# A DeepFM and CIN scorer on one core: six row buffers, gathers that wait for buffers alone, and three lookups instead of four in half of the tiles

## The chip, the cores and the metric

The kernel runs on one core of a Trainium2 chip. The metric is the device time of one execution in microseconds (us), the median of several runs. TensorE (PE in the profile), VectorE (DVE), ScalarE (ACT), GpSimd (POOL) and the DMA queues of SyncE (SP) work side by side and meet at semaphores.

## The reference

For each of 2048 samples there are 26 fields with an index each; an index picks a row of 16 numbers (`emb`) and one weight (`w1`) from the field's table of 12500 rows. Three scores are added:

```
emb = embed_table[f, x_idx]                      # 2048 x 26 x 16
lin1 = w1_table[f, x_idx].sum(1) + w1_bias
s = emb.sum(1);  fm = 0.5 * ((s*s).sum(-1) - (emb*emb).sum((1, 2)))
h = relu(emb.reshape(n, 416) @ mlp_w1 + mlp_b1)  # 416 -> 400
h = relu(h @ mlp_w2 + mlp_b2);  mlp_out = h @ mlp_w3 + mlp_b3
x0 = emb.transpose(0, 2, 1);  last = x0
for W in (cin_w0, cin_w1, cin_w2):               # 128 maps each
    last = einsum('ndl,ndf,klf->ndk', last, x0, W);  feats.append(last)
cin_result = concatenate(feats, -1).sum(1) @ lin_w + lin_b
out = lin1 + fm + mlp_out + cin_result           # 2048 x 1
```

## The kernel before

**Setup.** The three CIN layers are linear in their weights, so the kernel folds them with `lin_w` into one set of small matrices before it looks at any sample. This takes the first 80 us or so, with weight loads, small matmuls and round trips through DRAM.

**Tiles.** The 2048 samples are 16 tiles of 128, one sample to a partition. A tile needs its 26 rows of 17 numbers in `emb[t % EMB]`, with `EMB = 3` such buffers. They get there in two ways.

- *Gathers.* POOL issues one indirect DMA for each tile and field (L500), 128 rows each. Tiles 0 and 1 gather all 26 fields, tiles 2 to 15 the first 22: 360 gathers. The loop waits in three places. In tiles 0 and 1 some gathers wait for steps of the setup (`SETUP_STEPS`). From tile 3 on the first gather of a tile waits until the tile that held the buffer before has been copied (`by_pos_ready`) and its first-order weights summed (`row_sums`, ScalarE's L549 in `sum_first`). And from tile 2 on every second gather waits for `hi_ready`, a count of ScalarE's squares, so that tile t's gathers are spread over the units of tile t - 3 (`PER_UNIT`).
- *Lookups.* The last four fields of tiles 2 to 15 aren't gathered. Their whole tables lie in SBUF, 98 rows to a partition, split into a high and a low part (`look_hi`, `look_lo`, made in tile 0 by L617 and L923). For one lookup VectorE makes a one-hot matrix from the keys (L935), TensorE multiplies it with the tables in eight matmuls (L1197, L1198) into `ps_y`, and VectorE masks the right row (L946) and sums it into `emb` (L950). There are 56 lookups.

**A tile's compute.** ScalarE copies the 26 rows to `by_pos` (L568; for the last tile in parts, L556 and L561), TensorE transposes them in two halves (`x_half`), and then come 12 units, three to each of four quarters. In a unit TensorE forms sums of pairs of fields (`picked`, L1097), ScalarE squares them (L591, L598), VectorE takes the low part (L803), and TensorE multiplies three times (`main`, L1111 to L1113). The two layers of the MLP lie in between. Each engine has one queue, and its order is written out by hand in `tile(t)` and `start_tile(t)`. The position copy of tile t + 1 stands before unit 10 of tile t.

**Where the lookups stand.** A tile's compute has four slots for lookups: TensorE's part at units 0, 3, 6 and 9, VectorE's pick three units later, at units 3, 6 and 9 and in the next `start_tile`. `look_at(t, slot)` numbers the lookups through, shifted by `LATER = 2`: slots 0 and 1 of tile t hold fields 2 and 3 of tile t + 1, slots 2 and 3 hold fields 0 and 1 of tile t + 2. A pick into a buffer waits for the same two semaphores as the gathers.

Of the kernel before, what the change touches and what calls it, by code (L numbers as in the profile page):

```python
# [32 lines left out]
LOOKS = 4  # L33
FIRST_LOOK = 2
LATER = 2
EARLY = 18
PER_UNIT = 2
COLS = 98
WIDE = 26
SHARES = 4  # L40
# [57 lines left out]
def deepfm_cin_kernel(nc, x_idx, rows, w1_bias, mlp_w1, mlp_b1, mlp_w2, mlp_b2, mlp_w3, mlp_b3,  # L98
                      cin_w0, cin_w1, cin_w2, lin_w, lin_b, out):
    N, F = x_idx.shape  # L100
# [5 lines left out]
    T = N // P  # L106
# [13 lines left out]
    NC = 3  # L120
# [20 lines left out]
    with ExitStack() as ctx:  # L141
        def sb(name, shape, dt=F32):
            return ctx.enter_context(nc.sbuf_tensor(name, shape, dt))
# [4 lines left out]
        def sem(name):  # L148
            return ctx.enter_context(nc.semaphore(name))
# [16 lines left out]
        idx_wrap = sb("idx_wrap", [P, T, F])  # L166
        row_base = sb("row_base", [P, F], I32)
        row_ix = idx_raw
        EMB = 3
        emb = [sb(f"emb{t}", [P, F, R]) for t in range(EMB)]  # L170


# [152 lines left out]
        gathered_late = sem("gathered_late")  # L325
        by_pos_ready = sem("by_pos_ready")
        filled = sem("filled")
        hi_ready = sem("hi_ready")
# [19 lines left out]
        def s_no(t, u):  # L348
            return NPROD * t + NX + u

        def looks(t):

            return LOOKS if FIRST_LOOK <= t < T else 0

        def look_no(t, i):
            return LOOKS * (t - FIRST_LOOK) + i

        def look_at(t, slot):

            n = LOOKS * t + slot - LATER  # L360
            return (FIRST_LOOK + n // LOOKS, n % LOOKS) if 0 <= n < look_no(T, 0) else None

        def looked_by(t):

            return min(max(LOOKS * t + 1 - LATER, 0), look_no(T, 0))


        LOOK_SPLIT = {3: 0, 5: 1, 7: 2, 9: 3}
# [114 lines left out]
        @block.gpsimd  # L483
        def _(pool):
            pool.iota(row_base[:], pattern=[[V, F]], base=0, channel_multiplier=0).then_inc(base_ready, 1)
            SETUP_STEPS = {16: (m_done, 1), 22: (b_done, 1), 34: (s_blocks, 1), 41: (by_row_done, 1), 47: (za_done, 1)}
            for t in range(T):
                if t < 2:
                    pool.wait_ge(ix_ready, t + 1)
                if t >= EMB:  # L490
                    pool.wait_ge(by_pos_ready, 2 * (t - EMB + 1))
                    pool.wait_ge(row_sums, t - EMB + 1)
                for f in range(F - looks(t)):
                    if F * t + f in SETUP_STEPS:
                        signal, value = SETUP_STEPS[F * t + f]
                        pool.wait_ge(signal, value)
                    if t >= EMB - 1 and f and f % PER_UNIT == 0:
                        behind = s_no(t - EMB, NC + f // PER_UNIT - 1) if t >= EMB else s_no(0, f // PER_UNIT)
                        pool.wait_ge(hi_ready, behind + 1)
                    pool.indirect_dma_start(emb[t % EMB][:, f, :], None, rows,  # L500
                                            bass.IndirectOffsetOnAxis(row_ix[:, t, f:f + 1], 0)
                                            ).then_inc(gathered[t] if t < T - 1 or f < EARLY else gathered_late, 16)

# [16 lines left out]
        def _(act):  # L520
# [31 lines left out]
            def copy_last_early():  # L552
                act.wait_ge(gathered[T - 1], 16 * EARLY)
                act.wait_ge(looked, look_no(T - 1, LOOKS))
                for fs in (slice(0, EARLY), slice(F - LOOKS, F)):
                    act.activation(by_pos[:, :, fs], emb[(T - 1) % EMB][:, fs, 0:D].rearrange("p f d -> p d f"), ACT.Copy)  # L556

            def copy_last_late():
                fs = slice(EARLY, F - LOOKS)
                act.wait_ge(gathered_late, 16 * (F - LOOKS - EARLY))  # L560
                act.activation(by_pos[:, :, fs], emb[(T - 1) % EMB][:, fs, 0:D].rearrange("p f d -> p d f"),  # L561
                               ACT.Copy).then_inc(by_pos_ready, 2)

            def copy_by_position(t):
                act.wait_ge(gathered[t], 16 * (F - looks(t)))
                if looks(t):
                    act.wait_ge(looked, look_no(t, LOOKS))
                act.activation(by_pos[:], emb[t % EMB][:, :, 0:D].rearrange("p f d -> p d f"),  # L568
                               ACT.Copy).then_inc(by_pos_ready, 2)
# [54 lines left out]
            def tile(t):  # L624
                for u in range(NC, NU):
                    if u == NU - 2 and t + 1 < T - 1:
                        copy_by_position(t + 1)
                    square(t, u)
                    if u == NU - 1 and t + 1 == T - 1:
                        copy_last_early()  # L630
                        copy_last_late()
                    if t == 0 and u in LOOK_SPLIT:
                        look_high(LOOK_SPLIT[u])
                    if t == 0 and u == 8:
                        second_high()
                    if u == 5:
                        hidden1(t)
                    if u == 7:
                        hidden1_high(t)
# [75 lines left out]
        def _(dve):  # L715
# [148 lines left out]
            def tile(t):  # L864
                for u in range(NC, NU):
                    q = u // NC - 1
                    if u % NC == 2:
                        times_left(t, q)
                    z_low(t, u)
                    if u == NU - 1 and t + 1 < T - 1:  # L870
                        x_low(t + 1, 0)
                    if u % NC == 2 and q:
                        add_product(t, q)
                    if u == 7:
                        hidden1_low(t)
                    if t == 0 and u - 2 in LOOK_SPLIT:
                        look_low(LOOK_SPLIT[u - 2])
                    if t == 0 and u == 10:
                        second_low()
                    if u in PICKED and look_at(t, PICKED[u]):  # L880
                        pick_row(*look_at(t, PICKED[u]))
                    if u in KEYS and look_at(t, KEYS[u]):
                        keys_to_one_hot(*look_at(t, KEYS[u]))
# [15 lines left out]
            def start_tile(t):  # L899
                if look_at(t - 1, LOOKS - 1):  # L900
                    pick_row(*look_at(t - 1, LOOKS - 1))
                x_low(t, 1)
                z_low(t, 0)
                if look_at(t, 0):
                    keys_to_one_hot(*look_at(t, 0))
                z_low(t, 1)
                times_third(t - 1)
                add_third(t - 1)
                times_left(t - 1, NQ - 1)
                z_low(t, 2)  # L910
                hidden2(t - 1)
                add_product(t - 1, NQ - 1)
                fold(t - 1)
# [10 lines left out]
                                  ALU.subtract).then_inc(look_lo_ready, 1)  # L924

            def keys_to_one_hot(t, i):
                if i == 0 and t == FIRST_LOOK:
                    dve.wait_ge(keys_first_in, 16)
                elif i == 0 and t in (FIRST_LOOK + 1, FIRST_LOOK + 3):
                    dve.wait_ge(keys_in[(t - FIRST_LOOK) // 2], 16)  # L930
                n = look_no(t, i)
                keys = key_first[:, i:i + 1, :] if t == FIRST_LOOK else key_row[:, t - FIRST_LOOK - 1, i:i + 1, :]
                if n >= 2:
                    dve.wait_ge(rows_out, n - 1)
                dve.tensor_tensor(one_hot[n % 2][:], keys.to_broadcast([P, SHARES, P]),  # L935
                                  share_row.unsqueeze(2).to_broadcast([P, SHARES, P]),
                                  ALU.is_equal).then_inc(one_hot_ready, 1)
# [84 lines left out]
        def _(pe):  # L1022
# [103 lines left out]
            def sum_products(t):  # L1126

                if looked_by(t + 1):
                    pe.wait_ge(looked, looked_by(t + 1))
                pe.wait_ge(folds, t + 1)  # L1130
                pe.matmul(ps_y[:, YCOL + t:YCOL + t + 1], folded[0:NROW, :], ones[0:NROW, :],
                          start=True, stop=True).then_inc(y_done, 1)
# [173 lines left out]
```

## Time and profile before

| | |
|---|---|
| time, median of 3 runs | 512.84 us (511.73 to 513.11) |
| span of the profiled execution | 694.2 us |
| the profiled execution's own time | its span; no other is given |
| mean granted TensorE clock | 0.863 of full speed |
| POOL | 356.6 us busy, 360 gathers |
| TensorE, VectorE, ScalarE | 510.3, 412.8 and 389.0 us busy |

The profile is one execution, and its span is longer than the timed runs. In its rows L12 is line 12 of the kernel; "idle before" is the engine's own idle time, with the instruction that ended it, and "remote" stands where the releasing instruction wasn't found near the semaphore's update. PE's starts and ends are partly modelled.

### The profile page before, as it was taken

Reading aid. Unit: us, or ns where it says so; the run is one execution under the profiler, and the core shown is the slowest. Engines: PE = TensorE matmul, PEld = TensorE weight load, DVE = VectorE, ACT = ScalarE, POOL = GpSimd, SP = SyncE. Lnnn points to the kernel's source line nnn. Section 1 sums busy time; section 2 is a strip of 40 time slices with the busy share of each in tenths; the row PEclk is TensorE's granted clock in tenths of the full one; section 3 lists DMA queues with packets and bytes.
Section 4 is the critical chain, followed back from the end, with each engine's and each line's share of the span. In section 5 each row is a group of like instructions: output and inputs, shape, how many; then the busy total and the mean of one; then the engine's idle time right before and its main releaser. Section 6 shows DMA issues by size and latency. Waiting matters only on the chain.

```text
span 694.2 us, 6825 instructions
## 1 busy us (share of the span) xinstructions
PE 510.3 (74%) x2235; PEld 415.1 (60%) x2235; DVE 412.8 (59%) x680; ACT 389.0 (56%) x759; POOL 356.6 (51%) x365
## 2 busy tenths in 40 slices
PE   2897918824696959588695959596886949599988
PEld 2865705723484838476574747475765737478666
DVE  6431227903475748376584847484765848478866
ACT  0321628604464847376574847484665748378875
POOL 6665666774465464637466454547374664510000
PEclk9995666975896979979798989899797979899999
DMA  8836434221111111202111111112021111100000
GB/s 176 163 21 117 88 62 103 7 7 5 5 6 7 4 6 4 7 4 8 5 6 5 5 6 6 6 4 8 3 9 5 6 5 5 6 3 1 0 1 0
DMA packets 21508, 15.57 MB, mean 22 GB/s; under 512 B 12790, under 2 KB 19811, under 8 KB 21347
## 3 DMA queue, kind: packets, MB, share of 16 engines
q0 software_dynamic: 11520, 3.16, 13.5%
q1 hardware_dynamic: 6949, 9.99, 5.9%
q10 hardware_dynamic: 3005, 2.01, 1.4%
q8 instruction: 18, 0.29, 0.2%
q14 instruction: 16, 0.12, 0.1%
HBM read 14.92 MB, written 0.21 MB: 22 GB/s over the span
## 4 chain that ended last, share of the span: by engine, by line
PE 28%; DVE 24%; another core or an unknown queue 18%; ACT 15%; issue 11%; DMA 3%; SPq 0%; DVEq 0%
DVE z_lo L803 5%; ACT ps_s L598 5%; ACT z_hi L591 4%; PE ps_y L1197 4%; PE ps_y L1198 3%; DVE ps_y L946 3%; DVE one_hot L935 3%; PE ps_s L1097 2%; DMA w_space<-cin_w 2%; DVE sums L829 2%; PE ps_q L1111 2%; ACT room_a L597 2%; DVE ps_q L814 2%; DVE emb L950 2%
## 5 line engine op out<-in xcount | busy, mean ns | idle before, releaser
L500 POOL DMA_INDIRECT emb<-rows,idx_raw x360 | 356.3, 990 | 253.7 <-issue 101.4
L803 DVE TENSOR_TENSOR z_lo<-ps_s,z_hi 128x512 fp32r<-128x512 f32 (+1 forms) x192 | 132.1, 688 | 138.9 <-ACT ps_s L598 87.6
L591 ACT ACTIVATE z_hi<-ps_s 128x512 fp32r<-128x512 f32 (+1 forms) x192 | 114.2, 595 | 171.9 <-remote 105.6
L1197 PE MATMUL ps_y<-look_hi,one_hot 128*128 128x442 f32 x224 | 92.6, 413 | 91.4 <-DVE one_hot L935 89.6
L598 ACT ACTIVATE ps_s<-ps_s 128x512 f32<-128x512 f32 (+1 forms) x192 | 113.5, 591 | 0.7
L1111 PE MATMUL ps_q<-z_lo,zw_hi 128*127 128x512 f32 (+1 forms) x192 | 86.9, 453 | 32.6 <-DVE z_lo L803 21.1
L1197 PEld LDWEIGHTS ps_y<-look_hi,one_hot 128*128 128x128 f32 x224 | 49.5, 221 | 101.0 <-DVE emb L950 57.1
L1198 PE MATMUL ps_y<-look_lo,one_hot 128*128 128x442 f32 x224 | 89.3, 400 | 0.0
L946 DVE SCALAR_TENSOR_TENSOR ps_y<-tables,look_place,ps_y 128x442 f32<-128x442 f32 x56 | 37.9, 677 | 78.6 <-remote 70.6
L1097 PE MATMUL ps_s<-xt,pick 128*128 128x512 f32 (+1 forms) x192 | 77.1, 414 | 8.6 <-ACT x L582 5.4
L1113 PE MATMUL ps_q<-z_hi,zw_hi 128*127 128x512 f32 (+1 forms) x192 | 78.9, 411 | 0.0
L1112 PE MATMUL ps_q<-z_hi,zw_lo 128*127 128x512 f32 (+1 forms) x192 | 78.9, 411 | 0.0
L1111 PEld LDWEIGHTS ps_q<-z_lo,zw_hi 128*127 128x127 f32 (+1 forms) x192 | 38.2, 199 | 54.9 <-issue 34.4
L1198 PEld LDWEIGHTS ps_y<-look_lo,one_hot 128*128 128x128 f32 x224 | 50.1, 224 | 4.6
L1097 PEld LDWEIGHTS ps_s<-xt,pick 128*128 128x128 f32 (+1 forms) x192 | 37.4, 195 | 18.9 <-issue 5.8
L574 ACT ACTIVATE xt<-ps_s 52x512 fp32r<-52x512 f32 x32 | 18.7, 592 | 45.4 <-remote 17.1
L1113 PEld LDWEIGHTS ps_q<-z_hi,zw_hi 128*127 128x127 f32 (+1 forms) x192 | 38.0, 198 | 9.4
L597 ACT ACTIVATE room_a<-ps_s 128x512 f32<-128x512 f32 x63 | 37.4, 593 | 5.9 <-DVE sums L814 5.9
L1112 PEld LDWEIGHTS ps_q<-z_hi,zw_lo 128*127 128x127 f32 (+1 forms) x192 | 38.5, 200 | 2.6
L593 ACT ACTIVATE z_hi<-ps_s 26x512 fp32r<-26x512 f32 x64 | 37.9, 592 | 0.8
L935 DVE TENSOR_TENSOR one_hot<-w_space,tables 128x512 fp32r<-128x512 f16 x52 | 36.1, 694 | 0.0
L950 DVE TENSOR_REDUCE emb<-ps_y 128x17 f32<-128x442 f32 x56 | 34.7, 619 | 1.9
(191 smaller groups left out, 765.0 us busy)
## 6 DMA issues: line engine op xcount, KB each, us to landing
emb<-rows,idx_raw POOLq DMA_INDIRECT x360
w_space<-rows SPq DMA_DIRECT2D x2, 728.9 KB
m_space<-rows SPq DMA_DIRECT2D x2, 728.9 KB
w_space<-key_scratch SPq DMA_DIRECT2D x1, 1408.0 KB
w<-cin_w SPq DMA_DIRECT2D x2, 416.0 KB, 4.8
w<-cin_w ACTq DMA_DIRECT2D x2, 416.0 KB, 7.6
w_space<-cin_w SPq DMA_DIRECT2D x2, 416.0 KB
w_space<-cin_w ACTq DMA_DIRECT2D x2, 416.0 KB
```

Source lines behind the costliest of these rows:

```text
L500: pool.indirect_dma_start(emb[t % EMB][:, f, :], None, rows, bass.IndirectOffsetOnAxis(row_ix[:, t, f:f + 1], 0)).then_inc(gathered[t] if ...
L591: act.activation(z_hi[0:k, c, :], ps[0:k, :], ACT.Square)
L598: act.activation(ps[0:k, :], ps[0:k, :], ACT.Square).then_inc(hi_ready, 1)
L803: z = dve.tensor_tensor(z_lo[0:k, u % NC, :], ps, z_hi[0:k, u % NC, :].bitcast(F32), ALU.subtract)
L935: dve.tensor_tensor(one_hot[n % 2][:], keys.to_broadcast([P, SHARES, P]), share_row.unsqueeze(2).to_broadcast([P, SHARES, P]), ALU.is_equa ...
L946: dve.scalar_tensor_tensor(by_place, place.unsqueeze(2).to_broadcast([P, WIDE, R]), look_place[:, t, i:i + 1], by_place, ALU.is_equal, ALU ...
L1097: pe.matmul(ps[0:CK[c], :], pick[:, e, c * P:c * P + CK[c]], xt[t % 2][:, 4 * h:4 * h + 4, :], start=True, stop=True).then_inc(filled, 1)
L1111: pe.matmul(ps, hi_w, lo_x, start=(c == 0), stop=False)
L1112: pe.matmul(ps, lo_w, hi_x, start=False, stop=False)
L1113: mm = pe.matmul(ps, hi_w, hi_x, start=False, stop=(c == NC - 1))
L1197: pe.matmul(o, one_hot[n % 2][:, j, :], look_hi[i][:, ws], start=(j == 0), stop=False)
L1198: mm = pe.matmul(o, one_hot[n % 2][:, j, :], look_lo[i][:, ws], start=False, stop=(j == SHARES - 1))
```

## The change

Three edits:

- `EMB` goes from 3 to 6, so a buffer is used again six tiles later. The waits for `by_pos_ready` and `row_sums` follow it (`t >= EMB`, `t - EMB + 1`), in the gathers and in the picks.
- The wait for `hi_ready` before every second gather is gone, with `PER_UNIT`.
- `looks(t)` is 3 for tiles 8 to 15 (`FEWER_FROM = 8`). Field 0 of the four is gathered there as a 23rd field; slot 2 of tiles 6 to 13 stays empty. The other slots hold what they held. There are now 368 gathers and 48 lookups. The functions that number lookups are rewritten for it, and the last tile's copies follow `looks(T - 1)`.

```diff
--- before.py
+++ after.py
@@ -33,8 +33,8 @@
 LOOKS = 4
 FIRST_LOOK = 2
 LATER = 2
+FEWER_FROM = 8
 EARLY = 18
-PER_UNIT = 2
 COLS = 98
 WIDE = 26
 SHARES = 4
@@ -166,7 +166,7 @@
         idx_wrap = sb("idx_wrap", [P, T, F])
         row_base = sb("row_base", [P, F], I32)
         row_ix = idx_raw
-        EMB = 3
+        EMB = 6
         emb = [sb(f"emb{t}", [P, F, R]) for t in range(EMB)]
 
 
@@ -350,19 +350,26 @@
 
         def looks(t):
 
-            return LOOKS if FIRST_LOOK <= t < T else 0
+            return 0 if not FIRST_LOOK <= t < T else LOOKS if t < FEWER_FROM else LOOKS - 1
+
+        def first_field(t):
+            return LOOKS - looks(t)
+
+        LOOK_SEQ = [(t, i) for t in range(FIRST_LOOK, T) for i in range(first_field(t), LOOKS)]
 
         def look_no(t, i):
-            return LOOKS * (t - FIRST_LOOK) + i
+            return len([x for x in LOOK_SEQ if x < (t, i)])
 
         def look_at(t, slot):
 
             n = LOOKS * t + slot - LATER
-            return (FIRST_LOOK + n // LOOKS, n % LOOKS) if 0 <= n < look_no(T, 0) else None
+            look = (FIRST_LOOK + n // LOOKS, n % LOOKS)
+            return look if n >= 0 and look in LOOK_SEQ else None
 
         def looked_by(t):
 
-            return min(max(LOOKS * t + 1 - LATER, 0), look_no(T, 0))
+            n = max(LOOKS * t + 1 - LATER, 0)
+            return look_no(FIRST_LOOK + n // LOOKS, n % LOOKS)
 
 
         LOOK_SPLIT = {3: 0, 5: 1, 7: 2, 9: 3}
@@ -494,9 +501,6 @@
                     if F * t + f in SETUP_STEPS:
                         signal, value = SETUP_STEPS[F * t + f]
                         pool.wait_ge(signal, value)
-                    if t >= EMB - 1 and f and f % PER_UNIT == 0:
-                        behind = s_no(t - EMB, NC + f // PER_UNIT - 1) if t >= EMB else s_no(0, f // PER_UNIT)
-                        pool.wait_ge(hi_ready, behind + 1)
                     pool.indirect_dma_start(emb[t % EMB][:, f, :], None, rows,
                                             bass.IndirectOffsetOnAxis(row_ix[:, t, f:f + 1], 0)
                                             ).then_inc(gathered[t] if t < T - 1 or f < EARLY else gathered_late, 16)
@@ -552,12 +556,12 @@
             def copy_last_early():
                 act.wait_ge(gathered[T - 1], 16 * EARLY)
                 act.wait_ge(looked, look_no(T - 1, LOOKS))
-                for fs in (slice(0, EARLY), slice(F - LOOKS, F)):
+                for fs in (slice(0, EARLY), slice(F - looks(T - 1), F)):
                     act.activation(by_pos[:, :, fs], emb[(T - 1) % EMB][:, fs, 0:D].rearrange("p f d -> p d f"), ACT.Copy)
 
             def copy_last_late():
-                fs = slice(EARLY, F - LOOKS)
-                act.wait_ge(gathered_late, 16 * (F - LOOKS - EARLY))
+                fs = slice(EARLY, F - looks(T - 1))
+                act.wait_ge(gathered_late, 16 * (F - looks(T - 1) - EARLY))
                 act.activation(by_pos[:, :, fs], emb[(T - 1) % EMB][:, fs, 0:D].rearrange("p f d -> p d f"),
                                ACT.Copy).then_inc(by_pos_ready, 2)
 
@@ -924,9 +928,9 @@
                                   ALU.subtract).then_inc(look_lo_ready, 1)
 
             def keys_to_one_hot(t, i):
-                if i == 0 and t == FIRST_LOOK:
+                if i == first_field(t) and t == FIRST_LOOK:
                     dve.wait_ge(keys_first_in, 16)
-                elif i == 0 and t in (FIRST_LOOK + 1, FIRST_LOOK + 3):
+                elif i == first_field(t) and t in (FIRST_LOOK + 1, FIRST_LOOK + 3):
                     dve.wait_ge(keys_in[(t - FIRST_LOOK) // 2], 16)
                 n = look_no(t, i)
                 keys = key_first[:, i:i + 1, :] if t == FIRST_LOOK else key_row[:, t - FIRST_LOOK - 1, i:i + 1, :]
```

## Rows read from the trace of the kernel before

**Rows 1.** The page: the span, and each engine's busy time.

```profile
span 694.2 us, 6825 instructions
...
PE 510.3 (74%) x2235; PEld 415.1 (60%) x2235; DVE 412.8 (59%) x680; ACT 389.0 (56%) x759; POOL 356.6 (51%) x365
```

**Rows 2.** Windows by tile, between row sums: length, engines' busy us (instructions), PEclk, DMA.

```profile
0.00:80.10 80.10, 57.35 (x237) 47.85 (x238) 31.65 (x63) 21.78 (x47) 48.88 (x54) 0.84 0.58 104
80.10:132.20 52.10, 31.69 (x124) 24.39 (x124) 28.36 (x37) 30.57 (x53) 36.72 (x34) 0.76 0.41 85
...
387.40:425.50 38.10, 28.31 (x130) 23.29 (x128) 24.47 (x41) 23.01 (x45) 21.28 (x22) 0.91 0.16 6
...
616.50:643.90 27.40, 26.31 (x130) 22.05 (x128) 24.15 (x41) 22.92 (x46) 0.00 (x0) 1.00 0.00 1
643.90:673.10 29.20, 26.82 (x124) 20.74 (x123) 22.59 (x39) 22.70 (x46) 0.00 (x0) 1.00 0.00 1
673.10:694.20 21.10, 16.96 (x89) 13.66 (x88) 12.58 (x23) 14.01 (x31) 0.00 (x0) 0.95 0.00 0
```

**Rows 3.** Waits over the span: who waited for whom, us, times, longest.

```profile
ACT z_hi L591 <- remote: 105.6, 18, 9.0
...
POOL emb L500 <- ACT first_all L549: 78.0, 11, 10.8
...
POOL emb L500 <- ACT ps_s L598: 57.1, 16, 4.4
```

**Rows 4.** Timelines of VectorE and TensorE, 400 to 428: start, us, instruction, idle before.

```profile
409.99 0.68 DVE L946 SCALAR_TENSOR_TENSOR ps_y<-tables,look_place,ps_y 128x442 f32<-128x442 f32 x1 [7.63 <-remote]
...
412.07 0.71 PE L1197 MATMUL ps_y<-look_hi,one_hot 128*128 128x442 f32 x1 [8.18 <-DVE one_hot L935]
...
421.66 0.37 PE L1197 MATMUL ps_y<-look_hi,one_hot 128*128 128x442 f32 x1
```

**Rows 5.** Timelines of POOL: the last gather of tile 1, then others.

```profile
83.84 0.94 POOL L500 DMA_INDIRECT emb<-rows,idx_raw  x1 [0.30 <-issue]
85.09 0.95 POOL L500 DMA_INDIRECT emb<-rows,idx_raw  x1 [0.30 <-issue]
...
407.74 0.95 POOL L500 DMA_INDIRECT emb<-rows,idx_raw  x1 [0.30 <-issue]
412.79 0.95 POOL L500 DMA_INDIRECT emb<-rows,idx_raw  x1 [4.11 <-ACT ps_s L598]
```

**Rows 6.** Timeline of ScalarE: position copies of tile 14 and of tile 15.

```profile
630.36 0.96 ACT L568 ACTIVATE by_pos<-emb 128x416 f32<-128x416 f32 x1
...
660.57 0.94 ACT L556 ACTIVATE by_pos<-emb 128x288 f32<-128x288 f32 x2
```

**Rows 7.** Timelines of TensorE and VectorE: a lookup, and what follows it.

```profile
398.52 0.36 PE L1197 MATMUL ps_y<-look_hi,one_hot 128*128 128x442 f32 x1
...
400.04 0.39 PE L1111 MATMUL ps_q<-z_lo,zw_hi 128*127 128x512 f32 x1
...
631.09 0.68 DVE L946 SCALAR_TENSOR_TENSOR ps_y<-tables,look_place,ps_y 128x442 f32<-128x442 f32 x1
631.79 0.62 DVE L950 TENSOR_REDUCE emb<-ps_y 128x17 f32<-128x442 f32 x1
632.33 0.68 DVE L935 TENSOR_TENSOR one_hot<-w_space,tables 128x512 fp32r<-128x512 f16 x1
632.93 0.68 DVE L803 TENSOR_TENSOR z_lo<-ps_s,z_hi 128x512 fp32r<-128x512 f32 x1
```

**Rows 8.** Timelines of VectorE and POOL: slow gathers.

```profile
100.13 1.83 POOL L500 DMA_INDIRECT emb<-rows,idx_raw  x1 [0.30 <-issue]
...
123.58 1.89 DVE L923 TENSOR_TENSOR look_lo<-m_space,look_hi 128x1666 fp32r<-128x1666 f32 x1
...
123.79 2.50 POOL L500 DMA_INDIRECT emb<-rows,idx_raw  x1 [0.30 <-issue]
...
392.25 1.43 POOL L500 DMA_INDIRECT emb<-rows,idx_raw  x1 [0.30 <-issue]
```

## The prediction

> **What bounds the kernel now.** I read the page's shares first. No engine is full: TensorE is busy 74% of the span, VectorE 59%, ScalarE 56%, POOL 51% [rows 1]. But the span is 694.2 us, while the three timed runs have a median of 512.84 us. No other time of the profiled execution is given, so its span is its own time, and 181.4 us of it must be explained before any sum is made. The reader is to see in the windows by tile where they are. A tile in mid-kernel, during which POOL gathers, takes 38.1 us. Tile 13, after the last gather, takes 27.4 us with nearly the same work: VectorE 24.2 us busy in it against 24.5, ScalarE 22.9 against 23.0 [rows 2]. The list of waits says where the 11 us go: ScalarE waits 105.6 us, in 18 pieces of up to 9.0 us, for TensorE results whose release is shown as "remote" [rows 3]. The timeline of such a piece shows VectorE idle for 7.63 us before the one-hot pick, and the granted clock of the matmul after it is down: 0.71 us for a matmul that otherwise takes 0.37 [rows 4]. Three engines stand still while POOL goes on issuing.
>
> **The undisturbed time.** I put the tiles together without those stops. Setup to the first row sum of tile 0 is 80.1 us; tile 13 is 27.4, tile 14 29.2, the rest 21.1 [rows 2]. Tile 0 also splits the lookup tables. Against tile 13 it has 4.2 us more VectorE and 7.7 us more ScalarE work [rows 2], so 31.6 to 35.1 us; I take 34. Tiles 1 to 13 at 27.4 make 356.2. The sum is 80.1 + 34 + 356.2 + 29.2 + 21.1 = 520.6 us. That is 7.8 over the timed median, and 173.6 under the profiled span: practically the whole difference to the timed runs is these stops, and I take the timed runs to have none. The 7.8 us I take as a common overestimate, mostly setup; I subtract it from every sum below. In an undisturbed tile TensorE is busy 26.3 of 27.4 us [rows 2]. So the chain of TensorE and VectorE is full, and this compute chain sets the 512.84.
>
> **The second chain: POOL.** Gathers that follow each other start 1.25 us apart (0.95 busy, 0.30 between), beside idle engines and beside busy ones [rows 5]. 22 of them make 27.5 us, as long as a tile. The profile hides this, because its tiles last 38 us. There POOL waits 78.0 us for freed buffers (the row sums of L549) and 57.1 us for the pacing on ScalarE's units [rows 3], and looks like an engine with room. In a timed run it starts tile 2 at about 85 us [rows 5], and tile 3 some 28 us later, long after its buffer was freed at 80. From there on each tile of gathers is some 28 us behind the moment its buffer comes free (tile 4 from about 140, buffer free at 80.1 + 34 = 114), and neither the buffer wait nor the pacing is reached. What remains is plain: 13 tiles (2 to 14) of 22 gathers, 286 x 1.25 = 357.5, from 85.1 gives 442.6; 2 us for the landing, an estimate of twice a gather's own 0.95 [rows 5], since no row shows it; then from the position copy of tile 14 to the end 694.2 - 630.4 = 63.8 us, without stops [rows 6]. That is 508.4, less 7.8: 500.6 us. POOL has 12 us to spare now, not the 11 us a tile that the profile suggests. Tile 14 is taken, not 15, since its copy stands 30.2 us before that of tile 15 [rows 6], longer than a tile of gathers.
>
> **The change, part by part.**
> *Six buffers.* Three more tiles of run-ahead. By the sum above no buffer is waited for in a timed run; worth nothing there. In the profile it removes the 78.0 us of POOL's waits. Its cover if POOL is quicker than I take: then it is what lets POOL bank a lead before tile 8.
> *No pacing past the setup.* 57.1 us of POOL's waits in the profile [rows 3], nothing in timed runs by the same reasoning. Behind each of these waits stand only further gathers, and nobody waits for them until a copy two tiles later. A cost could come from denser gathers in tiles 0 and 1; in timed runs they are already dense, so I take nothing.
> *One lookup less for each of tiles 8 to 15.* It is done two tiles earlier, in tiles 6 to 13: 8 x (8 matmuls, one one-hot, one pick, one reduce). On TensorE the group runs from 398.52 to 400.04, 1.52 us; on VectorE the pick, reduce and one-hot run from 631.09 to 632.93, 1.84 us [rows 7]. Since TensorE is full and VectorE nearly so, I take 1.55 a tile, bounds 1.5 and 1.84: 12.4 us (12.0 to 14.7). The compute chain then ends at 512.8 - 12.4 = 500.4 (498.1 at best).
> *One gather more for each of tiles 8 to 15.* Of these the seven of tiles 8 to 14 stand before the copy that counts: 7 x 1.25 = 8.8 us, none hidden once POOL binds. POOL's chain: 85.1 + 293 x 1.25 + 2 + 63.8 - 7.8 = 509.4 us.
> *The rest* (which slots the last copies read, the numbering of lookups) moves no work: the same three copies.
> The later chain wins: 509 us, 0.7% less. The compute chain gives up 12.4 us and POOL takes about 9 of them back, by being late where it had been early.
>
> **What gathers cost beside VectorE.** Not all gathers take 0.95 us. The one at 123.79 takes 2.50 us, beside a 1.89 us table split on VectorE, and about one a tile takes 1.43 [rows 8]. Four slow ones between 100 and 124 us, of 1.83 to 2.50 [rows 8], add about 4.9 us, and the twelve further tiles about 0.48 each, 5.8 us. Charged in full the present POOL chain is 511.3, still under 512.84, and the new one 520.1. I take the flat 1.25, since a slow one is only counted fully if no other slack remains, but keep 520 as the upper bound.
> The Trainium skill, "SBUF — State Buffer", section "SBUF: two separate sides", states that GpSimd can't write its descriptors while VectorE holds the shared port pair in certain operations, and blocks until that one ends. By this trace's 2.50 us gather the trace agrees. By the rule every tile keeps its slow gathers in a timed run as well, and the sum would be the 520, not the 509.
>
> **Rivals.**
> 1. *The full gain.* If a gather costs 1.22 us or less in an untraced run, 0.03 under the row (9 us over some 300), POOL's chain ends before 500.4 and compute decides: 500, or 498 at best. For it: tracing plainly stops three engines, so it may also slow the fourth. Against it: the 1.25 is the same beside idle engines, and from the first gathers on.
> 2. *Slower.* The slow gathers count in full: POOL binds at 515 to 520. It decides once a gather costs more than 1.27 us in the mean. For it: the rows of slow gathers, the rule, and the upper limit that the present time sets, 512.84 + 8.8 = 521.6. It is also what follows if the 7.8 us lie in the tiles and not in setup, for then POOL's chain keeps them: 517. Against it: the present chain would have to be within 4 us of binding by coincidence.
> 3. *No change*: the same mechanism between 1.26 and 1.27 us; 511.3 to 514.4.
> 4. *Dense gathers stop TensorE.* If the stops of [rows 4] come from gathers that run with no pause, and some reach timed runs, each costs up to 9 us: 515 to 530. For it: VectorE resumed at 409.99, 1.3 us after POOL's last gather before its pacing wait [rows 4, 5]. Against it: the present timed runs have dense gathers by my reckoning and no stops.
>
> **The numbers.** POOL binds with part of the gain left (501.5 to 511.3): 0.34. The full gain: 0.22. No change: 0.14. Slower by POOL's chain: 0.26. Slower by stops: 0.04. Forecast 509 us; its own range 503 to 514. The range for 8 in 10 runs from 499 to 519; it leaves out the best of the full gain, the top of rival 2 and most of rival 4. Faster by over 0.3%: 0.56; within 0.3%, about what a measurement of this kernel can tell from no change: 0.14; slower: 0.30.
>
> **What the profile after would show.** 368 gathers and not 360; L1197 192 times and not 224, L946 48 times. POOL's waits for L549 and for L598 gone, the gathers one unbroken row until POOL is six tiles ahead, so the last gather ends earlier in the traced span although there are more. Tiles free of gathers in 6 to 13, if there are any, at 25.9 us and not 27.4; if 27.4 stays, the lookup was hidden. If rival 4 holds, stops are longer or more frequent. What would make the prediction wrong: a gather time under 1.22 us or over 1.27 us, which the trace alone can't tell.

## The result: slower by 1.5%, and the profile after

The changed kernel takes 520.83 us (median of 4 runs, 518.29 to 521.62) against 512.29 us (4 runs, 511.39 to 513.11). The ratio is 1.0149, with a 95% interval of 1.0119 to 1.0179. I had forecast 509 us with a range of 499 to 519. What came is rival 2, to which I had given 0.26; the median lies 0.8 us above its 520. In the session of experiments 1 to 4 one execution of the kernel before took 1182.13 us and is left out of the ratios; what held it up isn't known.

The profile of the changed kernel has a span of 516.5 us. Its page shows the engines' shares and the chain that ended last:

```profile
PE 456.4 (88%) x2171; PEld 372.4 (72%) x2171; DVE 396.3 (77%) x656; ACT 386.6 (75%) x759; POOL 361.4 (70%) x373
...
POOL 61%; issue 20%; PE 7%; ACT 5%; DMA 3%; DVE 3%; SPq 0%; POOLq 0%; DVEq 0%
POOL emb L504 61%; DMA w_space<-cin_w 3%; PE ps_q L1039 2%; ACT ps_s L602 1%; ACT z_hi L595 1%; PE ps_q L1115 1%; DVE z_lo L807 1%; DVE m_space L762 1%; DMA idx_raw<-x_idx 1%; PE ps_y L1146 1%; ACT z_hi L597 0%; PE ps_q L1117 0%; PE ps_q L1116 0%; ACT room_a L601 0%; PE ps_y L1201 0%
```

POOL looks least busy of all, at 70%, and yet its gathers (now L504) are 61% of the chain that ended last, and much of the 20% "issue" are the gaps between them. Past the setup they are one row without a break. POOL's main wait, in us, times and longest:

```profile
POOL emb L504 <- issue: 111.2, 365, 0.3
```

The 111.2 us are 365 gaps of 0.3 us between gathers; the other three gathers wait in the setup, 2.8, 2.8 and 1.3 us. The waits for buffers and for the pacing of [rows 3], 78.0 and 57.1 us, are gone. Whom POOL holds up is seen on ScalarE's timeline, before the position copies of tiles 12 and 14 (now L572):

```profile
396.10 0.94 ACT L572 ACTIVATE by_pos<-emb 128x416 f32<-128x416 f32 x1 [3.17 <-issue]
...
453.64 0.94 ACT L572 ACTIVATE by_pos<-emb 128x416 f32<-128x416 f32 x1 [2.01 <-issue]
```

In the whole profile ScalarE is idle for 11.8 us before six of these copies. The profile names no releaser for that idle time ("issue"), but the last gather of tile 14 does:

```profile
450.57 0.94 POOL L504 DMA_INDIRECT emb<-rows,idx_raw  x1 [0.30 <-issue]
```

A gather lands 3.0 us after its start (the median of this profile, given at the end), here at 453.57, and the copy starts at 453.64. In [rows 6] the same instruction follows the square before it with no idle time. The windows by tile (tiles 5, 6, 8, 9 and 14; us, then busy us of PE, PEld, DVE, ACT and POOL) tell from where on it binds:

```profile
211.10:238.50 27.40, 26.33 (x130) 22.07 (x128) 24.14 (x41) 22.86 (x46) 20.91 (x22) 1.00 0.22 8
238.50:265.20 26.70, 25.10 (x122) 20.42 (x120) 22.52 (x38) 22.97 (x46) 20.09 (x22) 1.00 0.22 8
292.40:321.10 28.70, 25.42 (x122) 20.36 (x121) 22.56 (x38) 22.95 (x46) 21.69 (x24) 1.00 0.22 8
321.10:350.90 29.80, 26.72 (x123) 21.67 (x121) 22.51 (x38) 22.94 (x45) 22.49 (x25) 0.94 0.20 7
466.20:495.40 29.20, 26.85 (x125) 20.82 (x124) 22.62 (x39) 22.63 (x46) 10.68 (x12) 1.00 0.13 5
```

Tile 5, with four lookups, takes the 27.4 us of the undisturbed tile in [rows 2]. Tile 6, with one fewer, takes 26.7. From tile 8 on POOL sets the pace. The six tiles 8 to 13, from 292.4 to 466.2, take between 26.7 and 32.0 us and 29.0 on average; 23 gathers take 28.8 us at 1.25 each and 29.4 at the 1.28 measured below.

### The profile page after: what moved, and what is told of

Read it like the earlier page. It is cut to its first block, busy times and chain, and to the rows that moved or that the text cites. A ratio compares the mean times of both kernels' runs of the same rounds, so it can differ in the third digit from the quotient of the medians.

```text
span 516.5 us, 6650 instructions
## 1 busy us (share of the span) xinstructions
PE 456.4 (88%) x2171; PEld 372.4 (72%) x2171; DVE 396.3 (77%) x656; ACT 386.6 (75%) x759; POOL 361.4 (70%) x373
## 4 chain that ended last, share of the span: by engine, by line
POOL 61%; issue 20%; PE 7%; ACT 5%; DMA 3%; DVE 3%; SPq 0%; POOLq 0%; DVEq 0%
POOL emb L504 61%; DMA w_space<-cin_w 3%; PE ps_q L1039 2%; ACT ps_s L602 1%; ACT z_hi L595 1%; PE ps_q L1115 1%; DVE z_lo L807 1%; DVE m_space L762 1%; DMA idx_raw<-x_idx 1%; PE ps_y L1146 1%; ACT z_hi L597 0%; PE ps_q L1117 0%; PE ps_q L1116 0%; ACT room_a L601 0%; PE ps_y L1201 0%
## 5 line engine op out<-in xcount | busy, mean ns | idle before, releaser
L504 POOL DMA_INDIRECT emb<-rows,idx_raw x368 | 361.1, 981 | 118.2 <-issue 111.2
L1115 PE MATMUL ps_q<-z_lo,zw_hi 128*127 128x512 f32 (+1 forms) x192 | 82.8, 431 | 13.7 <-DVE z_lo L807 11.7
L1201 PE MATMUL ps_y<-look_hi,one_hot 128*128 128x442 f32 x192 | 71.4, 372 | 14.9 <-DVE one_hot L939 14.9
L1202 PE MATMUL ps_y<-look_lo,one_hot 128*128 128x442 f32 x192 | 68.7, 359 | 0.0
L1201 PEld LDWEIGHTS ps_y<-look_hi,one_hot 128*128 128x128 f32 x192 | 37.2, 194 | 20.1 <-issue 17.1
L1202 PEld LDWEIGHTS ps_y<-look_lo,one_hot 128*128 128x128 f32 x192 | 37.3, 194 | 2.9
L818 DVE TENSOR_TENSOR ps_q<-ps_q,room_a 127x512 f32<-127x512 f32 x47 | 32.2, 686 | 0.5 <-PE ps_q L1117 0.5
L833 DVE TENSOR_TENSOR sums<-ps_q,sums 127x512 f32<-127x512 f32 x47 | 32.2, 685 | 0.4
L950 DVE SCALAR_TENSOR_TENSOR ps_y<-tables,look_place,ps_y 128x442 f32<-128x442 f32 x48 | 32.3, 673 | 0.0
L954 DVE TENSOR_REDUCE emb<-ps_y 128x17 f32<-128x442 f32 x48 | 29.7, 619 | 1.7
```

The costliest lines, as they stand in the source:

```text
L504: pool.indirect_dma_start(emb[t % EMB][:, f, :], None, rows, bass.IndirectOffsetOnAxis(row_ix[:, t, f:f + 1], 0)).then_inc(gathered[t] if ...
L1115: pe.matmul(ps, hi_w, lo_x, start=(c == 0), stop=False)
L1201: pe.matmul(o, one_hot[n % 2][:, j, :], look_hi[i][:, ws], start=(j == 0), stop=False)
L1202: mm = pe.matmul(o, one_hot[n % 2][:, j, :], look_lo[i][:, ws], start=False, stop=(j == SHARES - 1))
```

## The experiments

Theory A is that POOL's unbroken row of gathers sets the end, so that each gather that is added or made slower before tile 14's copy is paid in full. Its rivals are that dense gathers disturb the other engines (B), and that POOL had room before, in which buffers count (C). Each ratio below is of a kernel's runs to those of the kernel before in the same session. The diffs are shortened; those of 2 and 3 are told against the kernel before, the others against the changed kernel, 5 with `FEWER_FROM = 16`.

**1. The kernel before, once more.** No edit.

> The kernel before, profiled once more, with nothing changed. Theory A (POOL's row of gathers binds after the change): the stops of 8 to 15 us in the first profile belong to that one execution; this profile has a span near 511 us, tiles of 27.4 to 28 us, POOL with nearly no waits for L549 or for the pacing, and its last gather near 475 us. Rival B (POOL has real room in the kernel before, and dense gathers are what cost time after): POOL waits several us in each tile for L549 or L598, as in the first profile. Ratio 1.00 under both.

Measured: 510.84 us, ratio 0.9977 (0.9954 to 1.0000), span 511.6 us. The stops are gone, and so is POOL's waiting. The last gather starts at 471.6 us, where I had expected about 475. The window of tile 10, and POOL's waits:

```profile
351.60:379.00 27.40, 26.32 (x130) 22.06 (x128) 24.14 (x41) 22.85 (x46) 20.91 (x22) 1.00 0.22 8
```

```profile
POOL emb L500 <- issue: 99.3, 326, 0.3
POOL emb L500 <- ACT ps_s L598: 8.8, 29, 0.3
POOL emb L500 <- PE ps_q L1035: 4.3, 1, 4.3
```

The 29 waits for L598 are 0.3 us each, no more than the usual gap between two gathers: the pacing is passed without a stop, and no wait for L549 is left. How little POOL had to spare is on two timelines of this profile, the last gather of tile 14 and the copy that needs it:

```profile
443.50 0.94 POOL L500 DMA_INDIRECT emb<-rows,idx_raw  x1 [0.30 <-issue]
```

```profile
447.72 0.95 ACT L568 ACTIVATE by_pos<-emb 128x416 f32<-128x416 f32 x1
```

With 3.0 us to landing, which is this profile's median too, 443.5 + 3.0 = 446.5: POOL was 1.2 us early at tile 14. The run also shows the size of the measurement's own noise: 0.23% between two groups of runs of one kernel.

**2. The buffers and the pacing alone.**

```diff
-        EMB = 3
+        EMB = 6
-                    if t >= EMB - 1 and f and f % PER_UNIT == 0:
-                        behind = ...
-                        pool.wait_ge(hi_ready, behind + 1)
```

> Six buffers and no pacing, with four lookups for every tile from 2 on: the first two edits alone, 360 gathers. Theory A: no buffer or pacing wait was reached before, so nothing moves: 510 to 513 us. Rival B: dense gathers slow the other engines: 518 us or more. Rival C (POOL had room and can now bank a lead): under 510 us.

Measured: 510.12 us, ratio 0.9963 (0.9946 to 0.9980). Within the noise that run 1 shows, nothing moved. Rival C's lead is not to be seen. Rival B is answered by run 1 more than by this one: the gathers of the kernel before were as dense already, so denser ones can't be what the change brought. In this profile, with a span of 508.1 us, POOL is 61% of the chain that ended last, and ScalarE is idle 0.7 and 1.2 us before the copies of tiles 13 and 14; in run 1's POOL is 10%. So which of the two chains ends last in a kernel with four lookups is decided within 1 or 2 us, and those lie in the setup: tile 0's compute ends at 104.9 us in run 1's profile and at 101.0 in this one, while tile 2's gathers start at 77.6 and 76.2.

**3. The lookups alone**, with three buffers and the old pacing.

```diff
-            return LOOKS if FIRST_LOOK <= t < T else 0
+            return 0 if not FIRST_LOOK <= t < T else LOOKS if t < FEWER_FROM else LOOKS - 1
```

> Three buffers and the old pacing, with three lookups for tiles 8 to 15: the third edit alone, 368 gathers. Theory A: as the whole change, 518 to 522 us, since the eight added gathers alone are late. Rival B: 500 to 512 us, the gain of the lookups without the cost of dense gathers. Rival C (the buffers carry the gathers): slower than the whole change, over 523 us.

Measured: 519.65 us, ratio 1.0129 (1.0095 to 1.0163). The third edit carries the whole loss, and the buffers neither cause it nor lessen it.

**4. The whole change without the added gathers.** Field 22 of tiles 8 to 15 is neither gathered nor looked up.

```diff
-                for f in range(F - looks(t)):
+                for f in range(F - LOOKS if t >= FIRST_LOOK else F):
```

> The whole change without the added gathers: field 22 of tiles 8 to 15 is neither gathered nor looked up, and the buffer's old row is used, so that the output is not the reference's. 360 gathers, 48 lookups. Theory A: POOL's row then ends 8 x 1.25 = 10 us earlier, and binds again or nearly: 508 to 511 us. If the compute chain had set the 512 us before, as predicted, and POOL had 12 us to spare: 500 to 502 us.

Measured: 508.15 us, ratio 0.9917 (0.9887 to 0.9947). Two things follow. The added gathers cost 1.0149 - 0.9917 = 2.3%, 11.9 us (by the two intervals, about 2 us more or less), where eight at 1.25 us make 10. Between the two profiled executions tile 15's first gather moves by 9.9 us and the span by 9.5. And taking eight lookups away for nothing gives only 0.8%, 4 us: POOL is on the chain again at once (60% of the chain that ended last).

**5 and 6. The compute chain by itself**, with four and with three lookups. Both have six buffers and no pacing, and only 19 gathers in each of tiles 8 to 15; the other fields keep old rows.

```diff
-                for f in range(F - looks(t)):
+                for f in range(F if t < FIRST_LOOK else F - LOOKS if t < 8 else F - LOOKS - 3):
```

> Six buffers, no pacing, four lookups in every tile from 2 on, and only 19 instead of 22 gathers in tiles 8 to 15; fields 19 to 21 of those tiles keep the buffer's old rows, so that the output is not the reference's. This frees the compute chain from POOL and shows its own length. Theory A: compute at 27.4 us a tile was just under POOL before, so 507 to 510 us. If compute had been hidden well under POOL: under 505 us.

> As the run with 19 gathers in tiles 8 to 15, but with three lookups there (the last of the four fields kept, the first left out with the gathers). The difference of the two is what the eight removed lookups are worth to a compute chain that waits for no gather. The prediction took 1.55 us each, 12.4 in all: 497 us. The undisturbed three-lookup tiles of the two profiles since (26.7 us against 27.4) say 0.7 us each, 5.6 in all: 503 us.

Measured: 510.44 us, ratio 0.9982 (0.9961 to 1.0002), and 506.16 us, ratio 0.9878 (0.9829 to 0.9926). A tile of each, the four-lookup one first:

```profile
375.80:403.20 27.40, 26.33 (x130) 22.06 (x128) 24.16 (x41) 22.90 (x46) 20.98 (x22) 1.00 0.22 8
```

```profile
374.20:400.90 26.70, 25.08 (x122) 20.41 (x120) 22.55 (x38) 23.00 (x46) 20.30 (x22) 1.00 0.22 8
```

With three gathers fewer in eight tiles the first is as slow as the kernel before, and by runs 1 and 2 POOL is at most about 1 us early or late there. So before the change compute and POOL both ended at 510 to 512 us. Both runs missed what I expected, by 0.4 us over the range and by 3 us over the 503; the lookups are worth 5.7 us in the two profiles and 5.3 (give or take 2.7) by the ratios. And a lookup less saves 0.7 us, though it takes 1.25 us of busy time from TensorE and 1.6 from VectorE.

**7. The one-hot with one SBUF input.** The changed kernel, with four comparisons with a scalar in place of one comparison of two tensors.

```diff
-                dve.tensor_tensor(one_hot[n % 2][:], keys.to_broadcast([P, SHARES, P]),
-                                  share_row.unsqueeze(2).to_broadcast([P, SHARES, P]),
-                                  ALU.is_equal).then_inc(one_hot_ready, 1)
+                for j in range(SHARES):
+                    hot = dve.tensor_scalar(one_hot[n % 2][:, j, :], keys[:, 0, :], share_row[:, j:j + 1], None,
+                                            ALU.is_equal)
+                hot.then_inc(one_hot_ready, 1)
```

> The changed kernel with the one-hot made by four comparisons with a scalar each, one SBUF input, and not by one comparison of two SBUF inputs. In the profile after, every slow gather past the setup stands beside a one-hot or a table split. Theory A: the slow gathers beside the one-hot go, 5 us over the 368, and since POOL binds the time falls by 3 to 5 us, to 515 to 518, although VectorE has more instructions. Rival (the slow gathers have another cause, or cost nothing): no change, or slower by the added VectorE work.

Measured: 515.26 us, ratio 1.0064 (1.0042 to 1.0086). Timelines of VectorE and POOL, first in the profile after, where a gather beside the one-hot takes 1.44 us:

```profile
374.76 0.68 DVE L939 TENSOR_TENSOR one_hot<-w_space,tables 128x512 fp32r<-128x512 f16 x1
...
374.81 1.44 POOL L504 DMA_INDIRECT emb<-rows,idx_raw  x1 [0.30 <-issue]
```

and in this run, where beside the four comparisons it takes 0.98:

```profile
303.65 0.86 DVE L940 TENSOR_SCALAR one_hot<-w_space,tables 128x128 fp32r<-128x128 f16 x4
...
303.95 0.98 POOL L504 DMA_INDIRECT emb<-rows,idx_raw  x1 [0.30 <-issue]
```

VectorE works longer for each one-hot, 0.86 us instead of 0.68, and a tile of four lookups takes 27.8 us instead of 27.4; yet the kernel is faster by 0.8%, 4.4 us. The 293 gathers of tiles 2 to 14 take 1.264 us each in this profile and 1.280 in the profile after, 4.7 us less in all. The slow gathers are real and are paid in full. What the run doesn't separate is whether the second tensor input or the length of one instruction (0.68 us against about 0.2) is what counts.

**8. No waits of POOL for the setup.**

```diff
-            SETUP_STEPS = {16: (m_done, 1), 22: (b_done, 1), 34: (s_blocks, 1), 41: (by_row_done, 1), 47: (za_done, 1)}
+            SETUP_STEPS = {}
```

> The changed kernel without the waits of POOL for five steps of the setup (4.1 us of idle in the profile after). Theory A: POOL's unbroken row starts its last part 4 us earlier and the end follows: 515 to 518 us. Rival (something in the tiles and not POOL's row sets the end): 520 to 521. Rival B: the gathers slow the setup's loads, and the compute start moves late: also 520 or more.

Measured: 514.72 us, ratio 1.0058 (1.0034 to 1.0081). An edit in the setup moves the end by 0.9%, 5 us. Compute did not start earlier by it: the row sum of tile 0 stands at 67.6 us, in the profile after at 65.8. What moved is POOL's row: its first gather of tile 2 starts at 71.7 us and not at 76.7, 5.0 earlier, with the same 1.28 us a gather after it.

**9. Three lookups from tile 12 on.**

```diff
-FEWER_FROM = 8
+FEWER_FROM = 12
```

> The changed kernel with three lookups only for tiles 12 to 15: 364 gathers. Theory A (POOL's row sets the end, each gather before tile 14's copy costs its 1.25 us): four gathers fewer than the whole change, 5 us off: 514 to 517 us. If buffers, pacing or anything else of the change set the time: 519 or more. If the compute chain set it, this kernel would be slower than the changed one.

Measured: 516.46 us, ratio 1.0073 (1.0037 to 1.0109): 0.76% under the whole change, 3.9 us for four gathers. The interval is wide (1.5 to 6.3 us), and the profiled execution, 518.23 us, is the second longest of this run's seven.

**10. Runs 8 and 9 together.**

> Six buffers, no pacing, no waits of POOL for the setup, and three lookups for tiles 12 to 15. Theory A: POOL's chain ends at 514.7 less 4 x 1.25, 509.7 us; the compute chain, 510.4 less 4 x 0.7, at 507.6; the later one binds: 508 to 511 us, as good as or slightly better than either kernel.

Measured: 510.74 us, ratio 0.9972 (0.9953 to 0.9991). It lies in the range I expected, and it is level with run 1, the unchanged kernel at 0.9977. No complete version that I tried is shown to beat the kernel before.

## Why the prediction was wrong, point by point

- **The stops belong to one execution.** Right. Run 1 profiles the same kernel at 511.6 us, and 173.6 of the 181.4 us had been put down to them.
- **The common overestimate of 7.8 us lies in setup.** Right in the main. POOL starts tile 2 at 77.6 us in run 1's profile and at 76.7 in the profile after, and not at 85.1 [rows 5]: 7.5 and 8.4 earlier. The compute chain's setup and tile 0 end at 104.9 us in run 1, where I had 80.1 + 34 = 114.1: 9.2 earlier. An undisturbed tile is 27.4 us in all of them.
- **Buffers and pacing are worth nothing.** Right (run 2), and so was the reason: POOL is never stopped by them (run 1).
- **POOL's chain.** The mechanism was right, and its other terms were off by less than 1 us each. The step that failed is "I take the flat 1.25": the term of 293 gathers at 1.25 us was mis-sized. These are the first gather of tile 2 and the first of tile 15 in the profile after:

```profile
76.67 0.94 POOL L504 DMA_INDIRECT emb<-rows,idx_raw  x1 [0.30 <-issue]
...
451.82 0.94 POOL L504 DMA_INDIRECT emb<-rows,idx_raw  x1 [0.30 <-issue]
```

  The 293 gathers between take 375.2 us, 1.28 each, where I had 366.3. Nineteen of them take more than 0.97 us, 1.01 to 2.60, and are together 9.3 us over the usual 0.944. With the measured terms the sum reads 76.7 + 375.2 + 1.8 (to the start of the copy at 453.6) + 62.9 (to the end) = 516.6, the span (516.5). I had 77.3 + 366.3 + 2 + 63.8 = 509.4. Of the difference of 7.2 us the gathers are 8.9, and the rest goes the other way. The forecast was for the timed median, which came 11.4 us above it: the rest is 1.8 us between a profile's span and that execution's time (518.29), and 2.5 between this execution, the fastest of the four, and their median. My full charge for slow gathers gave 520.1, 3.6 us over the span and 0.7 under the median; that close a fit to the median is partly luck, since the sum has no term for either of these two differences. The argument for the flat value was that a slow gather counts only if no other slack remains. But a row without a break has no slack; each delay in it is kept to the end.
- **The last 2.5 us.** The prediction has no term for what a late copy does to TensorE's clock. In run 3's profile, which is of the same gathers and lookups and was timed at 522.62 us, the copy of tile 14 comes after a longer wait, and what follows of tile 13 takes 14.8 us at a granted clock of 0.77, where it takes 12.6 at 1.00 in the profile after. First run 3's copy and window, then the window of the profile after:

```profile
455.71 0.95 ACT L576 ACTIVATE by_pos<-emb 128x416 f32<-128x416 f32 x1 [3.21 <-issue]
455.70:470.50 14.80, 13.70 (x57) 11.54 (x57) 9.52 (x15) 11.46 (x21) 11.14 (x13) 0.77 0.21 8
...
453.60:466.20 12.60, 11.24 (x56) 9.44 (x57) 9.51 (x15) 11.45 (x21) 9.55 (x11) 1.00 0.21 8
```

  Run 9's profile has the same, 15.0 us at 0.77. The three slower executions of the changed kernel have mean granted clocks of 0.977 to 0.984 against the profiled one's 0.989, which fits; no profile of one of them was taken, so for them it is not shown.
- **POOL has 12 us to spare in the kernel before.** Wrong by the same term, 286 gathers at 1.284 and not 1.25 us, 9.7 us; it had 1.2 us in run 1, and none in run 2. Charged in full my own sum had said 511.3, and that was the better reading.
- **The compute chain sets the time before.** Half right. It sets it (run 5), and POOL's chain sets it as well.
- **A lookup is worth 1.55 us a tile.** Wrong: 0.7 us (runs 5 and 6: from the row sum of tile 1 to that of tile 15 it is 385.3 and 379.6 us, 5.7 less over eight tiles). I took the engines' rows for the length of the chain, because TensorE was busy 26.3 of 27.4 us. The work removed was 1.52 and 1.84 us [rows 7], yet the tile shrank by less than half of it. My guess is that part of each tile's length are hand-overs between TensorE, ScalarE and VectorE, which a lookup partly fills; no run isolates them, and the cause stays open. Since POOL bound, this error did not reach the result. It shows that even the full gain, rival 1, was 506 and not 500 us.
- **Rival 4, dense gathers stop TensorE.** Not seen. In all eleven later profiles the gathers past the setup follow each other without a pause, and the span of each lies 1.8 us under that execution's own time.
- **The rule of the Trainium skill**, "SBUF — State Buffer", section "SBUF: two separate sides", pointed the right way: the slow gathers stayed in the undisturbed tiles. I gave it as a rival of 0.26; it should have been the forecast. The Trainium skill, in the same section, also lets a VectorE instruction with two SBUF inputs contend only with a GpSimd instruction that reads SBUF. A gather reads its row numbers (`idx_raw`) there, so the trace agrees. But further down in it the Trainium skill infers that `tensor_tensor` doesn't hold up the writing of descriptors, and here the gathers beside such a `tensor_tensor` were held up (1.44 us beside L939). The measurement decides; which part of a gather is held up the profiles don't show.

## What to carry to other kernels

Reckon a queue that runs without a break at its mean and not at its usual interval, held-up gathers included: over 293 gathers 0.03 us each came to 8.9 us, of the 11.4 us that the forecast missed by. Where a profile's span is far from the timed runs, idle time in it is no evidence of room: POOL's 135 us of waits in the first profile stood beside stops that the same kernel's second profile, timed at 513.37 us, doesn't have. And when two chains tie, moving work from one to the other loses unless the exchange rate is good; here a lookup gave 0.7 us to one chain and its gather took 1.25 us from the other.

## What the runs showed of the hardware

- Past the setup, slow gathers stand beside VectorE instructions with two inputs in SBUF alone, in every undisturbed profile: the splits of the tables (up to 2.7 us instead of 0.94), that of a weight matrix (1.0 to 1.14) and the one-hot (up to 1.47, by how much of it is left). Beside everything else that VectorE does there, most of it with an input in PSUM, no gather takes over 0.96 us, and beside the comparisons with a scalar of run 7 none over 1.01.
- Of a gather and a one-hot, the one that starts first isn't held up. In the ten undisturbed profiles other than run 7's, 342 gathers past the setup started before the one-hot beside them, and none took over 0.95 us. One that starts 0.05 to 0.09 us after it takes 1.41 to 1.46, one that starts 0.25 to 0.29 after it 1.20 to 1.23. Where the two start within 0.02 us of each other the gather takes 0.94 and the one-hot 0.72 to 0.75 instead of 0.68.
- A gather lands 3.0 us after its issue (2.9 to 7.8), though POOL is busy with it for 0.94 only. From the profile after:

```profile
DMA to landing us min/median/max: 2.9/3.0/7.8
```

- TensorE's granted clock fell after a wait for the gathers. In run 3's profile TensorE is idle for 2.49 us before its first matmul on tile 14's copy, and the clock granted from 455.7 to 461.7 us is 0.50, the lower of its two levels (1.2 of 2.4 GHz); in the profile after it is idle for 1.31 us at the same place, and the clock stays at 1.00.
- One profiled execution of the kernel before had stops of TensorE in nearly every tile, of 4 to 8 us from tile 3 on and of up to 13 before (I called them 8 to 15 in run 1's expectation), and its span was 181 us over the timed runs. The same kernel profiled again had none. What caused them stays open.
